# A two-layer decoder on one core: a projection moved around the gelu products, first keys and second rows moved, and the largest product taken from magnitudes

## The reference

```python
# block 1: gated recurrence over time, then a gelu network; y0 = layernorm(x), y = layernorm(y0)
q, k, v, g = y @ Wq + bq, y @ Wk + bk, y @ Wv + bv, sigmoid(y @ Wg + bg)   # 1024 columns each
state_t = decay * state_(t-1) + k_t * v_t;  out_t = g_t * q_t * state_t / 8
x2 = y0 + out @ Wo + bo
x = x + x2 + gelu(layernorm(x2) @ W1 + b1) @ W2 + b2
# blocks 2 to 5: cross attention (16 heads of 64), a product on 4-bit values,
# self attention (16 heads of 16), cross attention with one head
# block 6: every intermediate is rounded to 16-bit steps of its own largest magnitude
up, gate = qdq(qdq(z) @ dequant(w_up).T), qdq(qdq(z) @ dequant(w_gate).T)  # 768 columns
gate = qdq(gate * qdq_u16(sigmoid(gate)))
o = qdq(gate * up);  x = x + o @ dequant(w_down).T
```

## Time and profile before

| what | value |
|---|---|
| median of 3 runs | 1394.85 us (1392.35 to 1399.29) |
| the profiled execution, its own time | 1394.02 us |
| its span, first to last instruction | 1392.2 us |
| mean granted TensorE clock | 0.963 |
| busy: PE / PEld / DVE / ACT / POOL | 90% / 77% / 72% / 54% / 18% |
| the chain that ended last: PE / DVE / issue / ACT | 50% / 17% / 6% / 4% |

### The profile page before, as it was taken

How to read it: one execution, slowest core, us unless ns; L and a number is a source line. 1 busy time by engine, 2 the same in 40 slices (tenths; PEclk the granted TensorE clock), 3 DMA queues, 4 the chain that set the end, 5 groups by cost and what they waited for, 6 DMA issues and landing times.

```text
span 1392.2 us, 27638 instructions
## 1 busy us (share of the span) xinstructions
PE 1247.0 (90%) x9826; PEld 1071.0 (77%) x9826; DVE 1004.3 (72%) x2479; ACT 752.3 (54%) x1781; POOL 251.1 (18%) x338
## 2 busy tenths in 40 slices
PE   5999999979999999999999999999888999979518
PEld 4889888868788777887778778787677777769518
DVE  5975776656667777777777777777777985676984
ACT  5653535335655555555555555555545764425862
POOL 2433333326000000000000000000034444110100
PEclk9999999989999999999999999999999999989859
DMA  9200101041000000000000000000020003310001
GB/s 286 67 1 5 43 1 46 0 155 48 1 12 12 12 13 11 0 12 11 12 11 11 1 11 12 11 0 1 1 61 2 3 2 114 103 30 0 1 0 48
DMA packets 34547, 40.65 MB, mean 29 GB/s; under 512 B 4889, under 2 KB 29066, under 8 KB 34442
## 3 DMA queue, kind: packets, MB, share of 16 engines
q1 hardware_dynamic: 33614, 39.24, 9.1%
q10 hardware_dynamic: 828, 0.14, 0.1%
HBM read 35.36 MB, written 4.01 MB: 28 GB/s over the span
## 4 chain that ended last, share of the span: by engine, by line
PE 50%; DVE 17%; issue 6%; ACT 4%; POOL 1%; DVEq 0%; DMA 0%; SPq 0%; ACTq 0%; POOLq 0%
PE bank L791 8%; PE bank L793 7%; PE bank L792 7%; PE bank L1014 4%; PE bank L1004 3%; PE bank L996 3%; PE bank L972 3%; ACT prob L1695 2%; DVE nmx L2375 2%; DVE amax L2574 2%; PE bank L1248 2%; DVE kTl L2146 2%; PE bank L1386 1%; PE bank L1266 1%; DVE prob L2392 1%
## 5 line engine op out<-in xcount | busy, mean ns | idle before, releaser
L1695 ACT ACTIVATE prob<-bank,nmx 100x361 f32<-100x361 f32 x256 | 142.5, 560 | 202.9 <-DVE nmx L2375 198.8
L2375 DVE TENSOR_REDUCE nmx<-bank 100x1 f32<-100x361 f32 x256 | 124.1, 526 | 62.6 <-PE bank L996 61.6
L695 POOL TENSOR_TENSOR frstd<-fmoments,eps 100x1 f32<-100x1 f32 x32 | 6.2, 194 | 645.0 <-DVE fmoments L2318 645.0
L791 PE MATMUL bank<-cxTh,wxkh 128*128 128x362 f32 x256 | 99.9, 390 | 9.3 <-DVE kTl L2146 8.2
L2392 DVE TENSOR_SCALAR prob<-prob,rsum 100x361 f32<-100x361 f32 x256 | 92.9, 405 | 4.5
L1004 PE MATMUL bank<-ident,prob 100*128 100x100 f32 (+1 forms) x768 | 89.6, 252 | 0.6 <-DVE prob L2392 0.5
L1004 PEld LDWEIGHTS bank<-ident,prob 100*128 100x128 f32 (+1 forms) x768 | 84.5, 151 | 6.2 <-DVE prob L2392 1.9
L791 PE MATMUL bank<-wxvh,cxTh 128*128 128x512 f32 (+1 forms) x192 | 84.4, 440 | 1.6 <-DVE vv L2298 1.2
L793 PE MATMUL bank<-cxTh,wxkl 128*128 128x362 f32 x256 | 84.1, 329 | 0.0
L792 PE MATMUL bank<-cxTl,wxkh 128*128 128x362 f32 x256 | 83.8, 327 | 0.0
L1014 PE MATMUL bank<-pT,vv 128*64 128x100 f32 (+1 forms) x1536 | 81.5, 255 | 1.7 <-ACT pT L1689 0.6
(11 more groups left out here) (432 smaller groups left out, 3703.6 us busy)
## 6 DMA issues: line engine op xcount, KB each, us to landing
cx<-in_ctx_dram SPq DMA_DIRECT2D x32, 128.0 KB, 2.1
xc<-in_ctx_dram SPq DMA_DIRECT2D x32, 128.0 KB
parked_weights<-parking SPq DMA_DIRECT2D x9, 256.0 KB, 5.6
mask_i<-in_mask_BxS_ik_dram SPq DMA_DIRECT2D x16, 141.0 KB
w<-in_L_attn_W_dram SPq DMA_DIRECT2D x2, 1024.0 KB, 13.5
cx<-in_ctx_dram SPq DMA_DIRECT2D x16, 105.0 KB, 2.0
xc<-in_ctx_dram SPq DMA_DIRECT2D x16, 105.0 KB
x<-in_x_dram SPq DMA_DIRECT2D x4, 400.0 KB
```

The lines of the kernel that those rows point to most:

```text
L791: pe.matmul(o, wh, mh, start=start, stop=False)
L1695: nc.scalar.activation(prob[:, h % 4, :], bank[S_BANKS[e]][0:T, 0:S], ACT.Exp, bias=nmx[:, h:h + 1], accum_out=psum_[:, h:h + 1]).then_inc ...
L2375: nc.vector.tensor_reduce(nmx[:, h:h + 1], bank[S_BANKS[e]][0:T, 0:S], AX_X, ALU.max, negate=True).then_inc(xa_max, 1)
```

## The change

Four edits, and nothing else:

- **A.** The next group's fourth projection (step 3) no longer comes at its own turn. Its keys and gates go in front of the gelu loop, its values and queries between the last two `hidden_summed`.
- **B.** The transposes of the second rows, and ScalarE's copies of them, go from before the first tile to behind tile 1; the third and fourth stay behind tiles 3 and 8.
- **C.** `keys_projected(0)` goes from behind the last block product to the front of the last pair of heads.
- **D.** The largest final product is taken from magnitudes. ScalarE makes |UP| and |product| as int16 (`Abs` for `Copy`), one fused instruction per group (`tensor_tensor_reduce`) multiplies them on VectorE and keeps the maximum, in the group order 2, 3, 0, 1. The signed integers are then made on ScalarE in eight halves of a group (`integers(j)`), and the signed products by VectorE in the same eight (`weighted(j)`), both between the passes that follow the last factor. VectorE's `gates_widest(2)` and `gates_weighted(3)` move behind the last maxima of UP.

The diff with indentation cut:

```diff
--- before.py
+++ after.py
@@ -309,6 +309,8 @@
     gi = sb("gi", [P, KI, B * T], I16, scope=s2)
+    with ExitStack() as s3:
+        au = sb("au", [P, NG, KI, N], I16, scope=s3)
     su = sb("su", [P, 2, KI, N], U16, scope=s2)
@@ -317,6 +319,8 @@
     dnl = sb("dnl", [P, KI, D], F32R, scope=s2)
+    with ExitStack() as s3:
+        ag = sb("ag", [P, KI, N], scope=s3)
     ol = sb("ol", [P, KI, B * T], F32R, scope=s2)
@@ -444,6 +448,7 @@
 TILE_BANK = [i % 4 for i in range(2 * KI)] + [(0, 1, 2, 3, 6, 4, 5)[i % 7] for i in range(2 * TILES - 2 * KI)]
+ROWS_BEHIND = {1: 1, 3: 2, 8: 3}
 D_BANKS = (1, 2, 3, 4, 5, 6, 0)
@@ -908,14 +913,14 @@
     for c in range(2, KC):
-        if c > 2:
+        if c > (3 if g else 2):
             project(first + c, (0, 1))
...
             transposes(u0, SIDE_BANK0, l0_nt)
-        if c > 2:
+        if c > (3 if g else 2):
             project(first + c, (2, 3))
@@ -942,6 +947,7 @@
         project(first + KC + 2, (2, 3))
+        project(first + KC + 3, (0, 1))
     for c in range(KC):
@@ -955,6 +961,8 @@
     hidden_summed(first + KC - 2)
+    if follows:
+        project(first + KC + 3, (2, 3))
     hidden_summed(first + KC - 1)
@@ -1047,9 +1055,25 @@
               stop=True).then_inc(a1_rb, 1)
+def keys_projected(i):
+    o = bank[FIRST_BANKS[i]] if i < 2 else bank[QK_BANK]
+    if i == 1:
+        pe.wait_ge(a1_qb, 1)
+    if i > 1:
+        pe.wait_ge(a1_x, 2 * i - 3)
+    for c in range(KD):
+        for k in range(KD):
+            mm = pe.matmul(o[:, 2 * T * c:2 * T * (c + 1)], wk1[:, k, c * P:(c + 1) * P],
+                           zT[:, i, k, :], start=(k == 0), stop=(k == KD - 1))
+    mm.then_inc(a1_qk, 1)
 def pe_pair(i, n):
...
     final = ends and odd
+    if final and p == PAIRS0 - 1:
+        pe.wait_ge(xa_kl, LASTP)
+        keys_projected(0)
     at_least(pe, xa_exp, 2 * pair)
@@ -1175,19 +1199,6 @@
 block_product(B - 2)
-def keys_projected(i):
-    o = bank[FIRST_BANKS[i]] if i < 2 else bank[QK_BANK]
-    if i == 1:
-        pe.wait_ge(a1_qb, 1)
-    if i > 1:
-        pe.wait_ge(a1_x, 2 * i - 3)
-    for c in range(KD):
-        for k in range(KD):
-            mm = pe.matmul(o[:, 2 * T * c:2 * T * (c + 1)], wk1[:, k, c * P:(c + 1) * P],
-                           zT[:, i, k, :], start=(k == 0), stop=(k == KD - 1))
-    mm.then_inc(a1_qk, 1)
 def queries_projected(i):
@@ -1281,7 +1292,6 @@
     mm.then_inc(a1_pr, 1)
-keys_projected(0)
 queries_projected(0)
@@ -1429,12 +1439,11 @@
 row_transposes(0)
-row_transposes(1)
 pe.wait_ge(f1_w, 4)
...
     hidden_tile(i)
-    if i in (3, 8):
-        row_transposes(2 if i == 3 else 3)
+    if i in ROWS_BEHIND:
+        row_transposes(ROWS_BEHIND[i])
     if i == TILES:
@@ -1882,11 +1891,10 @@
 rows_high(0)
-rows_high(1)
 for i in range(TILES):
     hidden_out(i)
-    if i in (3, 8):
-        rows_high(2 if i == 3 else 3)
+    if i in ROWS_BEHIND:
+        rows_high(ROWS_BEHIND[i])
 nc.scalar.activation(sc[:, 47:48], sc[:, 40:41], ACT.Sigmoid)
@@ -1920,34 +1928,54 @@
 assert i == 2 * TILES
+def up_magnitudes(g):
+    nc.scalar.activation(au[:, g], group(up, g), ACT.Abs, scale=sc[:, 16 + UP:17 + UP]).then_inc(f1_ui, 1)
+def product_magnitudes(g):
+    nc.scalar.activation(group(gi, g), group(gt, g), ACT.Abs,
+                         scale=sc[:, 16 + PRODUCT:17 + PRODUCT]).then_inc(f1_pi, 1)
+def integers(j):
+    if j == 0:
+        act.wait_ge(f1_o, 3)
+    if j == 2:
+        act.wait_ge(f1_o, 4)
+    g, half = divmod(j, 2)
+    nc.scalar.activation(au[:, g, :, HALF * half:HALF * half + HALF], part_of(up, j), ACT.Copy,
+                         scale=sc[:, 16 + UP:17 + UP]).then_inc(f1_ui, 1)
+    nc.scalar.activation(part_of(gi, j), part_of(gt, j), ACT.Copy,
+                         scale=sc[:, 16 + PRODUCT:17 + PRODUCT]).then_inc(f1_pi, 1)
 act.wait_ge(f1_k, 2 * UP + 1)
-for g in range(NG):
-    if g == 0:
-        act.wait_ge(f1_p, NG)
-    if g == 1:
-        act.wait_ge(f1_p, NG + 1)
-    if g > 1:
-        act.wait_ge(f1_o, g - 1)
-    nc.scalar.activation(su[:, g % 2].bitcast(I16), group(up, g), ACT.Copy, scale=sc[:, 16 + UP:17 + UP]).then_inc(f1_ui, 1)
-    if g == 0:
-        act.wait_ge(f1_k, 2 * PRODUCT + 1)
-    nc.scalar.activation(group(gi, g), group(gt, g), ACT.Copy,
-                         scale=sc[:, 16 + PRODUCT:17 + PRODUCT]).then_inc(f1_pi, 1)
+act.wait_ge(f1_w, 4)
+up_magnitudes(2)
+up_magnitudes(3)
+act.wait_ge(f1_p, NG)
+up_magnitudes(0)
+act.wait_ge(f1_k, 2 * PRODUCT + 1)
+product_magnitudes(2)
+product_magnitudes(3)
+product_magnitudes(0)
+act.wait_ge(f1_p, NG + 1)
+up_magnitudes(1)
+product_magnitudes(1)
+integers(0)
+integers(1)
+integers(2)
 def rounded(j):
+    act.wait_ge(f1_o, NG + j + 1)
     nc.scalar.activation(part_of(up, j), part_of(up, j), ACT.Identity, scale=sc[:, 16 + OUTPUT:17 + OUTPUT],
...
 act.wait_ge(f1_k, 2 * OUTPUT + 1)
-act.wait_ge(f1_pi, NG)
-rounded(1)
 for j in range(1, PARTS):
-    if 1 < j < PARTS - 1:
-        rounded(j + 1)
+    rounded(j)
+    if j + 2 < PARTS:
+        integers(j + 2)
     act.wait_ge(f1_r, j)
     nc.scalar.activation(part_of(oh, j), part_of(up, j), ACT.Identity, bias=sc[:, 41:42]).then_inc(f1_hi, 1)
-    if j == 1:
-        rounded(2)
 @block.vector
@@ -2667,27 +2695,39 @@
 gates_weighted(2)
-gates_widest(2)
 link(ups_widest(14, TILES))
 widest_of(UP, TILES, 2 * TILES)
+gates_widest(2)
+scales(UP, P, unit_e12)
 gates_weighted(3)
-scales(UP, P, unit_e12)
 link(gates_widest(3))
...
 output_unit = unit_of(OUTPUT, (PRODUCT, UP), None)
-for g in range(NG):
-    dve.wait_ge(f1_ui, g + 1)
-    dve.wait_ge(f1_pi, g + 1)
-    nc.vector.tensor_tensor(group(up, g), group(gi, g), su[:, g % 2].bitcast(I16), ALU.mult).then_inc(f1_o, 1)
-    dve.wait_ge(f1_o, g + 1)
-    ins = widest(group(up, g), 52 + g)
-link(ins)
+for n, g in enumerate((2, 3, 0, 1)):
+    dve.wait_ge(f1_ui, n + 1)
+    dve.wait_ge(f1_pi, n + 1)
+    ins = nc.vector.tensor_tensor_reduce(ag[:], group(gi, g), au[:, g], 1.0, 0.0, ALU.mult, ALU.max,
+                                         accum_out=amax[:, 52 + g:53 + g])
+    ins.then_inc(f1_o, 1)
+    dve.wait_ge(f1_o, n + 1)
 widest_of(OUTPUT, 52, 52 + NG)
+def weighted(j):
+    g, half = divmod(j, 2)
+    dve.wait_ge(f1_ui, NG + j + 1)
+    dve.wait_ge(f1_pi, NG + j + 1)
+    cols = slice(HALF * j, HALF * (j + 1))
+    nc.vector.tensor_tensor(up[:, :, cols], gi[:, :, cols], au[:, g, :, HALF * half:HALF * (half + 1)],
+                            ALU.mult).then_inc(f1_o, 1)
+weighted(0)
 scales(OUTPUT, P, output_unit[1])
 dve.wait_ge(f1_k, 2 * OUTPUT + 1)
+dve.wait_ge(f1_o, NG + 1)
 first = slice(0, HALF)
@@ -2707,11 +2747,15 @@
 low_part(0)
+weighted(1)
 scale_back(OUTPUT, output_unit[0])
+weighted(2)
 low_part(1)
...
     residual(2 * j + 1)
+    if j + 3 < PARTS:
+        weighted(j + 3)
     if j + 2 < PARTS:
```

## The result

The changed kernel takes 1368.97 us (median of 4 runs, 1368.36 to 1369.26) against 1393.6 us of the kernel before (median of 4 by then, 1389.58 to 1399.29): ratio 0.983, 95% interval 0.981 to 0.9851. The forecast was 1369.9 us. The profiled execution has a span of 1367.5 us against 1392.2.

A forecast was written before the change was run, and what follows sets the result against it. TensorE, 90% busy, was taken to bound the kernel, with a few regular waits and clock falls. A 17.4 + B 0.8 + C 1.3 + D 4.6 = 24.1 us off 1394.0 gave 1369.9 us; range 1363 to 1380, the forecast's own 1366 to 1373.

The forecast's parts named there:

- The waits: First block, groups 0 to 2: TensorE's six waits before first gelu products and last gelu sums are covered, 12.4 us.
- four half-clock stretches: First block: four 3.3 us stretches of TensorE at half clock run at full clock once waits are filled, 6.5 us.
- the new wait: First block, sums' way back at the next group's third step: TensorE waits for ScalarE's copies, 0.5 us three times.
- rival 1: First block: the clock falls elsewhere, not hanging on a wait alone; 6.5 us are missing, 1376.4 us; chance 0.12.
- up to 1252.3, and the second rows' transposes about 0.6 more: Last block, B: two tiles at the lower clock end at 1252.3, then second rows' transposes at 1252.9; B 0.8 us.
- 0, if the clock rises later: Last block: lower bound of B's gain, against the 0.8 us taken.
- ScalarE's round: Final products' tail: rounding, high part and two more passes take 4.94 us a piece on ScalarE, against TensorE's 4.23.
- half of the gain given back: Final tail, D: output's factor 9.3 us earlier, but ScalarE's integers in its queue leave 4.6 us.
- Rival 2: D's fused VectorE pass costs product plus reduction, 5.3 us: 9.7 us more, 1379.6 us; chance 0.11.
- three such sums: Final tail, time per piece: ScalarE 4.94 us, TensorE 4.23, VectorE 3.8, so ScalarE sets the pace.

The follow-up runs named there:

- uncounted matmuls: Kernel before, with the matmuls that A moves computed once more, for nothing, where A puts them: 1389.49 us, ratio 0.9996.
- the last run: Changed kernel with high parts before conversions, four high parts on VectorE and matmuls for nothing before tail and gate tiles, but second rows' transposes ahead of tile 0: 1365.21 us.
- unfused: Changed kernel with the fused VectorE pass taken apart into a product and a reduction of the same length: 1380.03 us, ratio 0.9908.
- warmed: Changed kernel with high part ahead of conversions, fourth piece's conversions ahead of the output's factor, and 50 and 18 matmuls for nothing around it: 1368.26 us, ratio 0.9827.
- its two halves: Changed kernel with only keys and gates moved, ahead of the gelu products (1379.39 us) or of the last gelu sums (1378.93 us); queries and values back in the next group.
- high part first: Changed kernel with ScalarE's high part directly behind its rounding, a later piece's int16 conversions behind both: 1368.77 us, ratio 0.9829.
- the last two: Changed kernel with reordered conversions, four high parts on VectorE, matmuls for nothing before tail and gate tiles: 1362.07 us; the same with edit B undone: 1365.21 us.

## Why the prediction was right

**The total**: 24.1 us forecast, 24.7 in the spans and 24.6 in the medians. That it fits so closely is in part luck: A brought 2.3 us more in this pair of traces, B 0.7 less, and C with the self-attention behind it 0.1 instead of 1.3.

**A (17.4 forecast, 19.7 in the profile).** The waits went as forecast, 12.4 us in six, and so did the four half-clock stretches: both are gone from the profile, and the uncounted matmuls and the table above show that filling the waits is enough. Small terms made the difference. "I take 0.5, three times: 1.5 us" for the new wait was too much: four waits last 0.9 us. Two short waits that I left as they were got shorter by 1.2 us together: for kv (0.8 to 0.2), and one of 0.6 for x that is gone. In the last group the clock fell later: from its output sums to its first gelu product it is 11.51 us instead of 12.51. And up to the first output sums the changed kernel was 0.4 us behind (74.26 against 73.83). 17.4 + 0.6 + 1.2 + 1.0 - 0.4 = 19.8, of 19.7 measured. What the forecast did not say is that the 6.5 us belong to one execution. By the medians A is 15.6 us, with about 3 for the clock, and rival 1's "it does not hang on a wait alone" was partly right: of 18 open waits in four traces ten brought a stretch, never without a wait.

**B (0.8 forecast, 0.1 in the profile, nothing when undone).** The step that failed is "up to 1252.3, and the second rows' transposes about 0.6 more". The tiles ran at the lower clock as forecast, 4.1 us, but so did the transposes, 1.5 us from start to end instead of about 0.9, and the start of tile 2. The named lower bound, "0, if the clock rises later", is what came. With the clock up the order is worth about 0.4 us by itself, by the estimate from the last run.

**C (1.3 forecast).** The block product comes 19.31 us earlier than before, the queries 20.66: C is 1.35 us. The clock fell just when the keys stood in the gap: they took 2.46 us and still fitted. The mechanism is thus seen at its place, but its worth in the whole time is not shown: undone, C costs 3.5 us in the median with overlapping intervals, and the clock moves the stages around it by more than 1.35 us from trace to trace (table below).

**D (4.6 forecast).** From the products' factor to the last result it is 9.29 - 4.71 = 4.6 us. Each step is found: fused passes of 2.66 us, the output's factor 9.3 us earlier, ScalarE's round 4.85 us (4.94 forecast), half of the gain given back. Rival 2's price was right for what it named, a pass that costs product and reduction: taken apart, it is 10.0 us more, 9.7 forecast. The rows show 2.66 us for 2400 pairs of int16 with a running maximum, as for the product alone. By the Trainium skill (Vector Engine (DVE) Microarchitecture Reference, Points that are easy to get wrong) an operation of the scalar-tensor-tensor kind with two SBUF sources that are not bf16 has half the throughput, with no read port left for the accumulator. The fused pass, which the trace names `CUSTOM_DVE_ANT_0`, shows no such loss (2.66 us with the running maximum, 2.66 without); whether the rule is meant for this form no run here shows.

**Given back elsewhere.** Self-attention and the cross-attention behind it took 0.9 us longer, which no term had. Busy time by stretch, of the kernel before and then of the changed one (TensorE's busy time, granted clock, the DMA engines' share, GB/s):

```profile
1013.00:1100.00 87.00, 78.43 (x1020) 0.94 0.09 26
```

```profile
993.00:1080.00 87.00, 77.92 (x1005) 0.92 0.09 25
```

The mean clock of the 87 us behind the first queries is 0.92 instead of 0.94. All traces together show that this stage and the one before it go by the clock (distances in us; the first landmark is the last group's first gelu product):

| traces | clock, 15 us up to the first queries | first landmark to queries | clock, 45 us behind them | queries to first rows' transposes |
|---|---|---|---|---|
| changed kernel, B undone, unfused, warmed | 0.89 to 1.00 | 704.9 to 705.8 | 0.85 | 232.9 to 233.3 |
| D undone | 0.81 | 705.3 | 0.88 | 231.8 |
| A undone, its two halves, high part first, the last two | 0.68 to 0.70 | 707.1 to 708.0 | 0.87 to 0.88 | 231.7 to 232.2 |
| no C: kernel before, uncounted matmuls | 0.77 | 706.1, 706.6 | 0.89 | 232.2, 231.8 |
| no C: C undone | 0.54 | 709.3 | 0.85 | 233.0 |

Behind the queries the five traces at 0.85 take 232.9 to 233.3 us, the nine others 231.7 to 232.2: the 0.9 us are the clock's. Both distances together are 938.2 us before and 938.1 in the changed kernel, and 937.1 to 940.0 in the eleven traces with C, so that C's 1.35 us can't be told from the clock there. What decides where the clock falls stays open; it does not follow the edits.

## What to carry to other kernels

Count a wait of the engine that sets the path at its length, and the clock that it can cost on top as a range with both ends, since that part changes from execution to execution. When work is taken from one engine and spread over others, sum the round of each engine for one piece: the forecast of D came out of three such sums (4.94, 4.23, 3.8), and so did the next improvement, which moves 0.8 us of work a piece to the engine with the shortest round. Bring TensorE's clock up only where TensorE sets the pace.

## What was not expected of the hardware

- Matmuls for nothing in a wait can bring time back: 72 of them in the first block, and it was 4.95 us shorter in the profiled execution, with the clock at 1.00 instead of 0.97, though the timed executions hardly show it. Ahead of the gate's tiles 33 of them made the stage 2.9 us shorter.
- The scatter of this kernel is the clock's. The kernel before ran between 1388.2 us (mean clock 0.967) and 1397.7 us (0.960) on one chip, and over its 44 executions beside the experiments the time goes with the mean clock (correlation -0.94). The changed kernel's four runs lie between 1368.4 and 1369.3 us; that its scatter is smaller is not shown, since with B undone four runs spread over 3.6 us.
- A product and a running maximum in one VectorE pass over int16 sources cost what the product costs (2.66 us for 2400 elements), and 0.08 us for reading the accumulator.
- ScalarE's high part directly behind the rounding that it reads makes the round 0.14 us longer than with two other passes in between (4.99 against 4.85 us).
